# A decoder layer on one core: the negated row maximum of the softmax made on VectorE instead of GpSimd, and what is left on GpSimd in another order

## The reference, cut to what matters

```python
def _L0_attn_ref(x, Wq, Wk, Wv, Wo):              # 16 heads of 32
    q, k, v = ((x @ W).reshape(B, T, H, Dh) for W in (Wq, Wk, Wv))
    scores = jnp.einsum('bthd,bshd->bhts', q, k)
    scores = scores * jnp.tril(jnp.ones((T, T)))  # multiplied: a masked score is 0, not -inf
    attn = jax.nn.softmax(scores / T ** 0.5, axis=-1)
    return jnp.einsum('bhts,bshd->bthd', attn, v).reshape(B, T, H * Dh) @ Wo
...
x = x + _L0_attn_ref(_layernorm(x), Wq, Wk, Wv, Wo)
x = x + _L0_xattn_ref(_layernorm(x), ctx_1024, xWq, xbq, xWk, xbk)
x = x + _L0_ffn_ref(_layernorm(x), gate, up, down)    # 4-bit weights with scales, MLP of 4096
```

## Time and profile before

| | us |
|---|---|
| median of 3 runs (1622.73 to 1623.76) | 1622.83 |
| the profiled execution | 1622.83 |
| span of its profile, first to last instruction | 1621.1 |
| PE busy in the span | 1521.6 |
| DVE, ACT, POOL busy | 849.2, 550.2, 170.2 |
| POOL's shift L498, 256 times | 51.7 |

### The profile page before, as it was taken

One profiled execution on the slowest core, in us unless ns is written; L12 is line 12 of the kernel. 1 busy time (PEld: TensorE's weight loads), 2 busy tenths in 40 slices (PEclk: granted clock), 3 DMA queues, 4 the chain that ended last, 5 costly groups with the idle time before them and its releaser, 6 DMA issues.

```text
span 1621.1 us, 29653 instructions
## 1 busy us (share of the span) xinstructions
PE 1521.6 (94%) x9280; PEld 766.4 (47%) x9280; DVE 849.2 (52%) x1896; ACT 550.2 (34%) x1323; POOL 170.2 (10%) x446
## 2 busy tenths in 40 slices
PE   5968988998898979999999999999999999999998
PEld 3446446545644644444444444444444444444443
DVE  6467558567747874554444345444445444534222
ACT  4369249427815941222212122222211212221111
POOL 1624004103301660000000000000000000000000
PEclk8989999999999999999999999999999999999999
DMA  6542332142244330311121121111112112111111
GB/s 195 161 129 61 114 112 68 59 130 91 71 115 116 105 92 1 107 57 41 40 81 40 40 78 44 40 62 59 40 40 81 40 40 81 40 40 52 52 52 52
DMA packets 73553, 118.41 MB, mean 73 GB/s; under 512 B 10096, under 2 KB 54384, under 8 KB 68848
## 3 DMA queue, kind: packets, MB, share of 16 engines
q1 hardware_dynamic: 73456, 117.20, 22.9%
HBM read 93.32 MB, written 23.86 MB: 72 GB/s over the span
## 4 chain that ended last, share of the span: by engine, by line
PE 68%; issue 18%; DVE 4%; ACT 3%; POOL 2%; DMA 2%; SPq 2%; POOLq 0%; ACTq 0%; DVEq 0%
PE bank L549 21%; PE bank L550 21%; PE bank L551 21%; ACT prob L899 1%; POOL nmx L498 1%; PE bank L625 1%; DMA qk_dram<-qk 1%; POOL pk L491 1%; PE bank L606 1%; DVE w_split L1340 1%; PE bank L562 1%; SPq L321 1%; DMA xb<-in_L_xattn_bk_dram 1%; DMA pk_in<-L_ffn_down_W_packed_dram 0%; PE bank L595 0%
## 5 line engine op out<-in xcount | busy, mean ns | idle before, releaser
L549 PE MATMUL bank<-xf,ring 128*128 128x512 f16 x1024 | 388.3, 379 | 0.0
L550 PE MATMUL bank<-xf,ring 128*128 128x512 f16 x1024 | 388.1, 379 | 0.0
L551 PE MATMUL bank<-xf,ring 128*128 128x512 f16 x1024 | 388.1, 379 | 0.0
L1271 DVE SCALAR_TENSOR_TENSOR inter<-bank,col,gel 128x512 f32<-128x512 f32 x128 | 95.9, 750 | 377.9 <-PE bank L551 377.7
L549 PE MATMUL bank<-ring,hid 128*128 (+1 forms) x512 | 194.1, 379 | 4.2 <-DVE o_t L1137 1.8
L979 ACT CAST hid<-inter 128x512 f16<-128x512 f32 x128 | 79.2, 619 | 347.8 <-DVE inter L1271 332.0
L550 PE MATMUL bank<-ring,hid 128*128 (+1 forms) x512 | 194.0, 379 | 0.0
L551 PE MATMUL bank<-ring,hid 128*128 (+1 forms) x512 | 194.0, 379 | 0.0
L975 ACT ACTIVATE gel<-bank,col 128x512 f32<-128x512 f32 x128 | 87.9, 687 | 300.6 <-PE bank L551 300.5
L1152 DVE CUSTOM_DVE_ANT_0 bank<-bank,mask,col 128x128 f32<-128x128 f32 (+3 forms) x256 | 139.3, 549 | 37.4 <-PE bank L595 33.1
L551 PEld LDWEIGHTS bank<-xf,ring 128*128 (+1 forms) x1024 | 100.2, 98 | 120.9 <-issue 0.3
(11 more groups left out here) (142 smaller groups left out, 1837.4 us busy)
## 6 DMA issues: line engine op xcount, KB each, us to landing
xf<-xf_dram SPq DMA_DIRECT2D x32, 1024.0 KB, 5.0
stack<-qk_dram SPq DMA_DIRECT2D x128, 128.0 KB, 3.2
sc_in<-scale_t SPq DMA_DIRECT2D x32, 384.0 KB
qk_dram<-qk SPq DMA_DIRECT2D x32, 256.0 KB, 3.0
packed_t<-pk_t SPq DMA_DIRECT2D x32, 192.0 KB, 2.2
pk_in<-packed_t SPq DMA_DIRECT2D x32, 192.0 KB
X<-in_x_dram SPq DMA_DIRECT2D x4, 1024.0 KB, 6.6
pk_in<-L_ffn_gate_W_packed_dram SPq DMA_DIRECT2D x16, 256.0 KB, 2.7
```

The source lines that it names most:

```text
L549: pe.matmul(o, lhs(0), rhs(0), start=first, stop=False)
L550: pe.matmul(o, lhs(0), rhs(1), start=False, stop=False)
L551: return pe.matmul(o, lhs(1), rhs(0), start=False, stop=stop)
L1271: nc.vector.scalar_tensor_tensor(inter[:, q], bank[2 * q + 1][:], C_I, gel[:, q], ALU.mult, ALU.mult).then_inc(int_out, 1)
```

## The change

Three edits. The shift becomes a `tensor_scalar` by -1.0 on DVE, behind the small step of the same j; the tile `zero` and its memset go. `row_max` loses its wait for the shift two units back, since both now are on one engine. On POOL, `out_tail` comes first in a unit, `masked_values` is asked for in its own unit instead of the next one, and the three casts stand together behind it.

```diff
@@ POOL
-            def shift(n, u, j):
-                pool.wait_ge(max_done, n * ROWS + 4 * u + j + 1)
-                if u >= 2:
-                    pool.wait_ge(exp_done, n * ROWS + 4 * (u - 2) + j + 1)
-                    pool.wait_ge(e_zero_done, beyond_units(n, u - 2))
-                nc.gpsimd.tensor_tensor(nmx[:, u % 2, j:j + 1], zero[:], mx[:, u % 2, j:j + 1], ALU.subtract).then_inc(shift_done, 1)
...
                 for u in range(UNITS):
                     r, i = u // TT, u % TT
-                    shift(n, u, 0)
-                    shift(n, u, 1)
-                    if u > 0 and i > 0:
-                        masked_values(n, u - 1)
-                    if i > 1:
-                        convert(n * (NB // B) + r, r, 3 * i - 6)
-                    shift(n, u, 2)
-                    if i > 1:
-                        convert(n * (NB // B) + r, r, 3 * i - 5)
-                        convert(n * (NB // B) + r, r, 3 * i - 4)
-                    shift(n, u, 3)
                     if i == 2 and r > 0:
                         out_tail(n, r - 1)
+                    if i < TT - 1:
+                        masked_values(n, u)
+                    if i > 1:
+                        for a in range(3 * i - 6, 3 * i - 3):
+                            convert(n * (NB // B) + r, r, a)
                     if last and u in beside:
                         dequant_part(*beside[u])
@@ DVE
             def row_max(n, u, j):
                 i = u % TT
-                if u >= 2:
-                    dve.wait_ge(shift_done, n * ROWS + 4 * (u - 2) + j + 1)
                 alone(dve, s_full, n * ROWS + 4 * u + j + 1)
...
+            def shift(n, u, j):
+                dve.wait_ge(max_done, n * ROWS + 4 * u + j + 1)
+                nc.vector.tensor_scalar(nmx[:, u % 2, j:j + 1], mx[:, u % 2, j:j + 1], -1.0, None, ALU.mult).then_inc(shift_done, 1)
@@ DVE, between the batches
                     for j in range(AHEAD):
                         row_max(n + 1, 0, j)
+                        shift(n + 1, 0, j)
@@ DVE, in a unit
                         if h >= 0 and h % 4 == 0:
                             divide(n, h // 4)
+                        if u > 0 or j >= AHEAD:
+                            shift(n, u, j)
                         if j == 0 and u % TT == 1 and u > TT:
                             repacked(n, u // TT - 1)
```

More of the change, by code:

```diff
@@ L174, in decoder_layer @@
         nmx = sb("nmx", [P, 2, 4], F32)
-        zero = sb("zero", [P, 1], F32)
         x_nm = sb("x_nm", [P, 4], F32)
@@ L445, in _ @@
             nc.gpsimd.memset(ones[:], 1.0).then_inc(const_ones, 1)
-            nc.gpsimd.memset(zero[:], 0.0).then_inc(const_ones, 1)
-            pool.wait_ge(const_ones, 2)
+            pool.wait_ge(const_ones, 1)
             nc.gpsimd.affine_select(out=mask[:], in_=ones[:], compare_op=ALU.is_ge, fill=0.0, base=3 * P,
```

## The result

| | before | after |
|---|---|---|
| median of the runs, us | 1622.78 (4 runs, 1619.28 to 1623.76) | 1646.05 (4 runs, 1642.74 to 1647.78) |
| ratio, with its 95% interval | 1 | 1.0148 [1.0128, 1.0168] |
| profiled execution: span, us | 1621.1 | 1644.9 |
| PE, DVE, ACT, POOL busy, us | 1521.6, 849.2, 550.2, 170.2 | 1526.4, 893.8, 560.6, 123.2 |

The changed kernel is 1.5% slower, where 1618.3 us and "faster" were forecast; the time lies far outside of the range, and beyond the dearest rival too. (The lines' numbers after the change are: row maximum L1135, shift L1142, exp L884, `all_tokens` L1157, `reciprocals` L1167, `divide` L1177, the copy `turned` L1149, POOL's cast L489, `v_zero` L499, `out_tail` L505, the repack L684.)

The account below looks back on a forecast made before the run. ACT was taken to pace steady attention groups, DVE the batch starts, with one DMA hole in batch 0. Terms: -8.0 + 3.3 + 0.8 + 0.5 - 1.1 = -4.5 us, so 1618.3 us; 80% range 1613.5 to 1628.

Parts of the forecast that it names:

- the dearest rival: Rival B, DVE becomes the bound in every group: 1638 us, chance 0.10.
- What bounds the kernel: Attention: ACT sets the pace in steady groups, DVE at batch starts; ACT's 8.35 us hole in batch 0 is a DMA's.
- Term 1: Batch 0: with the shift on DVE, ACT's hole closes and exp(5,0) moves from 115.08 to 107.1: -8.0 us.
- one of the signs of being wrong: POOL's first cast starting at another time than 103.4, since the -8.0 us hangs on the DMA landing as before.
- Term 2: On DVE, shifts cost a unit about 0.46 us, in units 1 and 2 about 0.55.
- The bounds of 0.06 and 0.25: Cost in us of one shift on DVE with all of the wait hidden, and with none hidden.
- Term 3: DVE's cost on the path: +0.5 us in steady groups, +3.3 at starts of batches 1 to 3, +0.8 between batches.
- Term 4: POOL's new order: `divide` of a group's first unit no longer waits for out_tail: -1.1 us.
- Rival A: On DVE, a shift has to wait for POOL's operations: +5.5 us, 1623.8 us, chance 0.27.
- Rival B: DVE becomes the bound in every group once shifts cost more than 0.17 us each: 1638 us, chance 0.10.
- Rivals C and D: C: repack or v_zero holds PE longer, 1622 us, chance 0.08. D: DVE's cost hidden everywhere, 1614.5 us, chance 0.10.
- The rule on drains: DVE's next operation waits for an empty pipe: each shift would cost 0.15 us, the sum about 1 us higher.

Follow-up runs that it names:

- the early load: Kernel before, shifts still on POOL, first packed weights' load issued ahead of the loop, each next at the end of a batch: 1613.03 us, ratio 0.9956.
- The two kernels with an added wait: Kernel before plus a VectorE wait ahead of each row maximum: on the last maximum 1645.55 us, on the maximum before it 1622.38 us.
- the kernel with the added wait: Kernel before, shifts on POOL, VectorE also waiting ahead of each row maximum on the one just before it: 1645.55 us, ratio 1.0158.
- three late shifts: Changed kernel, shifts of j = 0 to 2 issued behind the next row maximum, that of j = 3 ending its own row: 1628.15 us, ratio 1.0053.

## Why the prediction was wrong, step by step

- **What bounds the kernel** was read rightly: ACT in the steady groups, DVE at the starts, and one hole that belonged to a DMA.
- **Term 1, -8.0 us**: the mechanism is confirmed by the early load. Its 7.8 us lie near the term by luck in part: with no DMA to wait for, the term's own sum gives 111.6 - 101.8 = 9.8, and batch 0 got 9.1 shorter. In the changed kernel exp(5,0) came 115.08 - 109.42 = 5.7 us earlier and not 8.0, and 1.85 of that is the earlier start of the batch, so the change itself gave 3.8. (The casts started at 101.61 and not 103.4, one of the signs of being wrong that had been named; here it only followed the start.) The casts were done at 103.74 and were not the limit; PE came to the repack only at 107.99, since units 1 to 4 had taken 19.5 us. That DVE's loss earlier in batch 0 would be hidden did not hold.
- **Term 2, "the next row maximum 0.07 later"**: this is the step that failed. Start of the shift, 0.18 after the READ: right. Length of a shift: right (149 ns on average, below). The row maximum behind it: 0.25 us after the shift in the loop and 0.17 in batch 3, by the medians. I took 0.07 from rows 7, from small operations behind small operations, and applied it to an instruction that has a register step, a wait and a semaphore step in front. Rows 6 had shown 0.09 for that instruction only while nothing ahead of it waited. The bounds of 0.06 and 0.25 were for the shift alone, and left this out: from READ to row maximum it became 0.43 - 0.09 = 0.34 more at j = 2, where 0.16 had been taken and 0.25 was the upper end.
- **Term 3, +4.6 us in all**: the place at the starts was right, the size was not: units 1 and 2 of batches 1, 2 and 3 took 2.1, 2.2 and 1.2 us more and not 1.1, and the term had nothing for units 3 and 4, so that units 1 to 4 took 4.6, 3.0 and 1.6 more. A steady group got 1.1 to 1.3 us longer in the loop (1.8 in batch 3) and not 0.05, since its 2.70 us of slack in DVE were used up. Units 9 to 12, with the large layer norm parts, got 3.3 us longer in batch 1; I had no term for them, and in fact counted on a gain.
- **Term 4**: `divide` waits for `out_tail` no more, as forecast. What it gave back can't be seen in the units where DVE is late anyway.
- **Rival A** (the shift waits for POOL): no. POOL ran six casts from 101.61 to 103.74, and within them DVE has

```profile
102.99 0.14 DVE L1142 TENSOR_SCALAR nmx<-mx 128x1 f32<-128x1 f32 x1
```

  The group of all shifts (count, busy us, mean ns):

```profile
L1142 DVE TENSOR_SCALAR nmx<-mx 128x1 f32<-128x1 f32 x256 | 38.3, 149 | 2.1
```

  In the whole attention 68 shifts started while a POOL operation was running, each of 0.14 to 0.16 us. The rule in the Trainium skill that I had read as speaking for this rival ("VectorE: DVE Perf Modes", "What auto-detection actually checks") asks for outermost non-unit dimensions that are even or equal, and I had left out the word non-unit; a 128x1 operand has no such dimension, and the trace agrees with the reading that the rule does not reach it.
- **Rival B** (DVE becomes the bound) is what happened, in its place and at its price of 1.3 us for a steady group. Its point of decision, 0.17 us per shift, was passed: if the group is taken as DVE's alone, as rival B does, the shifts cost (16.47 - 12.44) / 16 = 0.25 us for each row, which is the upper end that rival B was worked out with. It had a chance of 0.10. Two things were wrong in it: "at j = 0 and 3 the wait is certainly covered" (the wait is, the row maximum's own preparation is not), and the starts and units 9 to 12, which it had left as they were; the time came to 1646 and not 1638.
- **Rivals C and D**: the casts held PE nowhere, and DVE's cost was nowhere hidden in full.
- **The rule on drains** ("VectorE: DVE Perf Modes", "The DRAIN you can't avoid") was weighed as +1 us. The same section reports that chained operations take as long with a semaphore after each as without. The two kernels with an added wait part here: a met wait was free, an unmet one on the engine's own last result cost 1.5%. The Trainium skill says in "Perfetto Trace Analysis", "Per-engine timelines" that a sequencer-only instruction does its waiting in the sequencer itself, which fetches the next one only afterwards. The trace of the kernel with the added wait agrees: at the place shown, the step of that wait is at 407.25, READ having ended at 407.21, then the register step at 407.31 and the semaphore step at 407.40. In the changed kernel the wait belongs to the shift, which is engine work and no case of that sentence; there too the register step came only 0.05 us after READ's end.

Shown: an unmet wait on the row maximum, with nothing else changed, costs in batches 1 and 2 what the change cost there, within 1 us; the same wait met costs nothing; a further step in the stream costs where the wait is unmet and hardly where it is met; a further small instruction costs nothing that can be told apart; and the register and semaphore steps, which ran ahead of READ's end at most places before, come behind it at every place after. Inferred: what fills the last 0.15 us, from the semaphore step to the row maximum. Open: how the 6.6 us of batch 3 divide, since the wait alone cost 2.5 there (65.44 against 62.95) and leaves fewer steps behind it; whether POOL's new order takes a part of the 1.0% by which three late shifts are behind the early load; and a shift without any wait, which was not tried since it would be a race.

## What to carry to other kernels

A step moved from a helper engine to the engine that makes its input turns a wait between engines into a wait on oneself, and an engine that waits for its own last result loses its lead in the instruction stream: price what stands behind the moved step, registers, waits and semaphore steps included, and not only the step. Put such a step where its input is already old, but not behind something that itself waits for another engine. And when a stall is a DMA's that reaches an engine through a queue, start the DMA earlier before you reorder the queue: here that took no more than moving a call, and gave all of the gain.

## What the runs showed of the hardware that I had not expected

- A semaphore step without engine work lengthens the gap by 0.09 us where VectorE's stream is not ahead (0.43 to 0.52 from READ to row maximum), and by 0.00 where it is (0.09 with and without; the time rose by 0.2% even so).
- The gap is wider in the loop than in batch 3, which is written out and has no register step: 0.43 against 0.34 us from READ to row maximum. In the loop the semaphore step starts 0.09 after the register step, and in batch 3 it starts where the register step would, 0.05 after READ's end, so the register step is the difference. The timeline of DVE in batch 3 of the changed kernel has 0.17 from shift to row maximum:

```profile
583.29 0.14 DVE L1135 DVE_READ_ACCUMULATOR2_ANT mx<- 128x1 f32 x1
583.47 0.15 DVE L1142 TENSOR_SCALAR nmx<-mx 128x1 f32<-128x1 f32 x1
583.64 0.36 DVE L1135 CUSTOM_DVE_ANT_0 bank<-bank,mask,col 128x128 f32<-128x128 f32 x1
```

- Operations on both engines in SBUF do not all meet. In the changed kernel a 128x4 step with two tensors in, which takes 0.16 alone, lasted until POOL's long operation ended (587.55 + 1.13 = 588.68; 587.02 + 1.65 = 588.67), while none of the 128x1 shifts did. The two rows, from the timelines of DVE and POOL:

```profile
587.55 1.13 DVE L1157 SCALAR_TENSOR_TENSOR den_all<-e_zero,den 128x4 f32<-128x4 f32 x1
...
587.02 1.65 POOL L479 TENSOR_TENSOR ring<-w_full,ring 128x768 f16<-128x768 f32 x1
```

- PE's granted clock fell where DVE was late: 0.83 in units 1 to 4 of batch 2, where it had been 0.92 before, with PE idle in 17.98 - 14.49 = 3.5 us of the stretch. DVE was busy for 16.85 of the 17.98 us, so there the clock followed the loss. But in unit 4 it made a loss of its own: the same unit took 5.11 us in batch 1, with the clock at 0.71, PE busy in 5.04 of them and DVE only in 3.26, and 3.51 us in batch 2, with the clock at 1.00. (The clock is a mean of its two levels, 1.2 and 2.4 GHz.) These 1.6 us are why units 1 to 4 cost more in batch 1 than in batch 2. The unit ahead, unit 3, had PE busy for 3.27 of some 4.95 us in both batches, so the traces don't show what decided it. What the clock cost in all was not tested:

```profile
253.86:258.97 5.11, 5.04 (x66) 3.86 (x63) 3.26 (x17) 3.38 (x15) 0.40 (x1) 0.71 0.15 43
405.10:408.61 3.51, 3.43 (x64) 2.54 (x62) 3.18 (x17) 3.27 (x16) 0.40 (x1) 1.00 0.22 63
```
